# Macaron block (MoE, Mamba, MoE): second MoE phase's row 1 routed inside its row 0, skip term put first, last output row in two halves

## What is computed

```python
x = x + 0.5 * ffn(layernorm(x))
x = x + mamba(layernorm(x))
x = x + 0.5 * ffn(layernorm(x))      # the same weights again

def ffn(x):                          # 16 experts and 2 shared ones, 128 -> 128 -> 128
    scores = sigmoid(x @ router_w.T) # bias, best 2 of 4 groups, best 4 experts in them, weights
    h = einsum('td,edf->etf', x, gate_w)
    u = einsum('td,edf->etf', x, up_w)
    y = einsum('etf,efd->etd', silu(h) * u, down_w)
    return sum_e y[e] * combine[:, e] + shared(x)

def mamba(x):                        # two convolutions with gelu, softplus, 16 states per channel
    h = dA[t] * h + dBu[t]           # scanned along the tokens
    y = sum_n h * C + u * D          # u * D is the skip term
    return concat(y, z) @ W_out
```

## Time and profile before

| | |
|---|---|
| runs | 932.56 us median (931.9 to 933.38) |
| the profiled execution | 931.41 us, its span 929.3 us |
| PE | 887.6 us busy (96%) |
| DVE | 733.9 us busy (79%) |
| POOL | 646.3 us busy (70%) |
| ACT | 576.0 us busy (62%) |
| granted TensorE clock, mean | 0.989 |

### The profile page before, as it was taken

One profiled execution on the slowest core, in us unless ns is written; L12 is line 12 of the kernel. 1 busy time (PEld: TensorE's weight loads), 2 busy tenths in 40 slices (PEclk: granted clock), 3 DMA queues, 4 the chain that ended last, 5 costly groups with the idle time before them and its releaser, 6 DMA issues. The chain is left out here.

```text
span 929.3 us, 12347 instructions
## 1 busy us (share of the span) xinstructions
PE 887.6 (96%) x3655; PEld 632.7 (68%) x3655; DVE 733.9 (79%) x1248; ACT 576.0 (62%) x1022; POOL 646.3 (70%) x471
## 2 busy tenths in 40 slices
PE   8899999999998999999999887789999999999997
PEld 7678778787766665355455433367878878788885
DVE  5969768777975468999999999956877787796664
ACT  6475565565553778888977594136557557555554
POOL 7658666675655456999999887546666667566665
PEclk9999999999999999999999998999999999999999
DMA  7632443333323223334444344243334343334430
GB/s 201 200 123 78 143 121 95 112 118 100 110 84 90 71 81 112 137 118 160 157 154 141 117 136 137 70 141 122 108 111 133 95 134 114 98 102 138 136 112 13
DMA packets 65587, 109.80 MB, mean 118 GB/s; under 512 B 8168, under 2 KB 24688, under 8 KB 65520
## 3 DMA queue, kind: packets, MB, share of 16 engines
q1 hardware_dynamic: 65520, 109.02, 37.5%
HBM read 106.10 MB, written 2.88 MB: 117 GB/s over the span
## 5 line engine op out<-in xcount | busy, mean ns | idle before, releaser
L654 POOL TENSOR_TENSOR act_lo<-act,act_hi 128x512 fp32r<-128x512 f32 x288 | 374.8, 1303 | 237.9 <-ACT act_hi L745 237.4
L738 ACT ACTIVATE bank<-bank 128x512 f32<-128x512 f32 x252 | 146.6, 582 | 234.5 <-PE bank L1035 226.1
L943 DVE TENSOR_TENSOR sg<-bank,c_ring 128x512 f32<-128x512 f32 x252 | 172.6, 685 | 105.0 <-ACT bank L738 103.8
L1031 PE MATMUL bank<-x_parts,w_hi 128*128 128x512 f32 x572 | 235.8, 412 | 9.7 <-DVE act L923 7.1
L923 DVE TENSOR_TENSOR act<-sg,bank 128x512 f32<-128x512 f32 x288 | 197.8, 687 | 48.7 <-PE bank L1035 33.6
L1035 PE MATMUL bank<-x_parts,w_hi 128*128 128x512 f32 x572 | 225.8, 395 | 0.0
L1032 PE MATMUL bank<-x_parts,w_lo 128*128 128x512 f32 x572 | 225.7, 395 | 0.0
L745 ACT ACTIVATE act_hi<-act 128x512 fp32r<-128x512 f32 x288 | 179.4, 624 | 1.2 <-DVE act L923 0.4
L1031 PEld LDWEIGHTS bank<-x_parts,w_hi 128*128 128x128 f32 x572 | 107.8, 188 | 44.7 <-DVE act L923 14.7
L1035 PEld LDWEIGHTS bank<-x_parts,w_hi 128*128 128x128 f32 x572 | 107.7, 188 | 25.4
L1032 PEld LDWEIGHTS bank<-x_parts,w_lo 128*128 128x128 f32 x572 | 108.0, 189 | 24.5 <-issue 2.6
(11 more groups left out here) (182 smaller groups left out, 1049.9 us busy)
## 6 DMA issues: line engine op xcount, KB each, us to landing
c_ring<-c_dram SPq DMA_DIRECT2D x252, 256.0 KB, 3.3
c_ring<-c_dram SPq DMA_DIRECT2D x64, 512.0 KB, 3.7
out<-x_sb SPq DMA_DIRECT2D x8, 256.0 KB, 2.7
x_sb<-in_L_attn_hidden_states SPq DMA_DIRECT2D x3, 512.0 KB, 6.0
stage<-in_L_ffn_gate_w SPq DMA_DIRECT2D x4, 256.0 KB, 4.7
stage<-in_L_ffn_up_w SPq DMA_DIRECT2D x4, 256.0 KB, 4.9
stage<-in_L_ffn_down_w SPq DMA_DIRECT2D x4, 256.0 KB, 5.4
c_dram<-c_rows SPq DMA_DIRECT2D x64, 8.0 KB, 1.9
```

The costliest lines, as they stand in the source:

```text
L654: self.nc.gpsimd.tensor_tensor(m["act_lo"][:, g % LAG], m["act"][:, g % ACTS], m["act_hi"][:, g % LAG].bitcast(FP32), ALU.subtract).then_i ...
L738: nc.scalar.activation(self.s_bank[:, g % 2], self.h_bank[:, g % 2], ACT.Silu).then_inc(self.sg_ready, 1)
L943: nc.vector.tensor_tensor(m["sg"][:, g % 2], silu, weight, ALU.mult).then_inc(self.w_done, 1)
L1031: nc.tensor.matmul(dst, m["w_hi"][:, k, n, :], x_hi, start=True, stop=False)
```

## The change

It does five things. (1) `dve_route(0, 2)` in the Mamba pairs becomes `dve_route(0, 1)`; scores and logits of row 1 leave with it. (2) Row 1 of phase 2 is routed as in phase 1, from block 3 on, with its logits and scores at block 2. (3) The table `SECOND_ROUTE`, now used by both phases, leaves blocks 6, 7 and 10 free and ends at block 16; in phase 2 the statistics of rows 2 and 3 move from block 1 to block 6. (4) The skip term stands before act(1). (5) The last output row is copied, turned, added and stored in two halves.

```diff
                 for g, _ in enumerate(f2.dve_blocks(dve)):
-                    if g == 1:
+                    if g < 2:
                         next(tail)
...
-FRONT_DVE = {41: 1, 43: 1, 45: 1, 54: 2, 55: 2, 56: 2, 57: 2, 58: 2, 59: 1, 60: 1, 61: 1, 62: 1}
+FRONT_DVE = {41: 1, 43: 1, 45: 1, 54: 2, 55: 2, 56: 2, 57: 2, 58: 1, 59: 1, 60: 1, 61: 1, 62: 1}
...
-SECOND_ROUTE = {3 + n: 2 if n < 3 else 1 for n in range(10)}
+SECOND_ROUTE = {3: 2, 4: 1, 5: 1, 8: 1, 9: 1, 11: 1, 12: 1, 13: 1, 14: 1, 15: 1, 16: 2}
...
-    PAIRED = {2: 6, 4: 37, 6: 73}, {2: 1, 4: 37, 6: 73}
+    HALVES = slice(0, SEQ // 2), slice(SEQ // 2, SEQ)
+    PAIRED = {2: 6, 4: 37, 6: 73}, {2: 6, 4: 37, 6: 73}
...
     def rows_before(self, r):
-        if self.p:
-            return r // 2
         return r if r < 2 else 1 + r // 2
...
         if rows is not None:
-            sp.wait_ge(self.x_added, BATCH)
-            sp.dma_start(rows[BATCH - 1], m["x_sb"][:, BATCH - 1]).then_inc(self.stored, 16)
-            sp.wait_ge(self.stored, 16 * BATCH)
+            for n in range(2):
+                tiles = slice(n * TT // 2, (n + 1) * TT // 2)
+                sp.wait_ge(self.x_added, BATCH + n)
+                sp.dma_start(rows[BATCH - 1][:, tiles], m["x_sb"][:, BATCH - 1, tiles]).then_inc(self.stored, 16)
+            sp.wait_ge(self.stored, 16 * (BATCH + 1))
...
-        self.act_scores(ae, 0, 2)
+        self.act_scores(ae, 0, 1)
...
-                if self.p == 0 and g == 2:
+                if g == 2:
                     self.act_scores(ae, 1, 1)
...
     def act_last(self, ae):
-        self.act_read_acc(ae, BATCH - 1)
+        if self.out is None:
+            self.act_read_acc(ae, BATCH - 1)
+            return
+        ae.wait_ge(self.down_done, BLOCKS)
+        ae.wait_ge(self.ot_ready, BATCH - 1)
+        for cols in self.HALVES:
+            self.nc.scalar.activation(self.m["out_t"][:, cols], self.acc[:, cols], ACT.Copy, scale=0.5
+                                      ).then_inc(self.acc_read, 1)
...
-        yield from self.dve_route(dve, 0, 2)
+        yield from self.dve_route(dve, 0, 1)
...
+        for n, cols in enumerate(self.HALVES):
+            x = self.m["x_sb"][:, BATCH - 1].rearrange("p t d -> p (t d)")[:, cols]
+            dve.wait_ge(self.ot_ready, BATCH + n)
+            self.nc.vector.tensor_tensor(x, x, self.last_banks[n][:, 0:SEQ // 2], ALU.add).then_inc(self.x_added, 1)
...
-        routing = self.dve_route(dve, 1, 1) if self.p == 0 else None
+        routing = self.dve_route(dve, 1, 1)
...
-                if self.p == 0 and g == 2:
+                if g == 2:
                     self.pe_logits(pe, 1, 1)
...
     def dve_tail(self, dve):
         self.dve_skip_term(dve, BATCH - 1)
+        yield
         self.dve_add(dve, BATCH - 1)
         yield
```

More of the change, by code:

```diff
@@ L544, in __init__ @@
         self.acc, self.misc = bank[3][:, 0, :], bank[3][:, 1, :]
+        self.last_banks = self.misc, self.h_bank[:, 0, :]
         self.misc_reader = None
@@ L915, in dve_last @@
     def dve_last(self, dve, src):
-        self.dve_add(dve, BATCH - 1, src)
+        if self.out is None:
+            self.dve_add(dve, BATCH - 1, src)
+            return
+        for n, cols in enumerate(self.HALVES):
+            x = self.m["x_sb"][:, BATCH - 1].rearrange("p t d -> p (t d)")[:, cols]
+            dve.wait_ge(self.ot_ready, BATCH + n)
+            self.nc.vector.tensor_tensor(x, x, self.last_banks[n][:, 0:SEQ // 2], ALU.add).then_inc(self.x_added, 1)
     def dve_act(self, dve, g):
@@ L950, in dve_blocks @@
                     self.dve_add(dve, i - 1, self.misc)
+                for _ in range(SECOND_ROUTE.get(g, 0)):
+                    next(routing)
                 if self.p == 0:
-                    for _ in range(SECOND_ROUTE.get(g, 0)):
-                        next(routing)
                     if g in (self.PAIRED[0][2], self.PAIRED[0][4]):
@@ L1016, in pe_down, with pe_transpose_last @@
                          skip_group_check=True).then_inc(self.down_done, 1)
+    def pe_transpose_last(self, pe):
+        nc, m = self.nc, self.m
+        for n, (dst, cols) in enumerate(zip(self.last_banks, self.HALVES)):
+            pe.wait_ge(self.acc_read, BATCH + n)
+            for t in range(TT // 2):
+                last = nc.tensor.transpose(dst[:, t * P:(t + 1) * P], m["out_t"][:, cols][:, t * P:(t + 1) * P], m["ident"][:, :])
+            last.then_inc(self.ot_ready, 1)
     def pe_transpose_out(self, pe, i, dst):
@@ L1074, in pe_front_pieces @@
         yield
-        self.pe_logits(pe, 0, 2)
+        self.pe_logits(pe, 0, 1)
         yield
@@ L1118, in pe_last @@
         self.onto_misc(pe, self.x_added, BATCH)
-        self.pe_transpose_out(pe, BATCH - 1, self.misc)
+        self.pe_transpose_last(pe)
 class Mamba:
```

## The result

The changed kernel takes **926.34 us** (median of four runs, 925.12 to 926.81) where the kernel before took 932.23 beside it: a ratio of 0.9933, 95% interval 0.9916 to 0.9951, so 6.2 us less (4.6 to 7.8); the two medians are 5.9 apart. Its profiled execution took 925.93 us with a span of 924.1, against 931.41 and 929.3. 923.5 was forecast: the sign and the range held, the size was 2.8 us too large.

The account below looks back on a forecast made before the run. PE bounds 616 to 918 us, DVE the last Mamba pairs. Terms -2.8 - 2.55 - 2.33 - 1.8 + 0.8 - 0.4 = -9.1 from the profiled 931.41 give 922.3; plus 1.15 to the median, 923.5, range 921 to 927.

Parts of the forecast that it names:

- Phase 1: Row 0 of phase 1: PE's six stalls waiting for DVE's acts shrink, gaining 2.8 us, from 1.8 to 3.4.
- if it meets nothing in its new place: Phase 1, row 0: piece 5, moved behind act(8), runs undelayed there, so act(9) starts at 40.1.
- Mamba pairs: Last Mamba pairs: routing one row instead of two shortens DVE's work, 2.3 us plus 0.25 for logits, 2.55 in all.
- rival 3: Mamba pairs: saved time isn't passed on because POOL or PE at lower clock sets the pace; loses 2, 925.5; chance 0.08.
- The idle 2.33: Between Mamba and phase 2: the skip term ahead of act(1) removes PE's idle time, gaining 2.33 us.
- Its clock: Projection behind the idle time: PE's granted clock no longer falls, gaining 1.8 us, or 0 if it falls all the same.
- rival 1: Projection between Mamba and phase 2: PE's clock stays down; gain 7.3, time 925.3; chance 0.18.
- Phase 2: Row 0 of phase 2: row 1's logits and route pieces give back 0.8 us, with 0.5 of stall, from 0 to 2.5.
- rival 2: Route pieces meet POOL in phase 2's blocks 3 to 6, also phase 1; waits cost 2.5 to 3, 926.0; chance 0.12.
- The end: Last output row in halves: stages overlap and the last store comes earlier, gaining 0.4 us, from 0 to 0.7.
- Weights of row 1: Phase 1: turned at block 16 instead of 12, their loads stay hidden by 1 us, cost 0.
- Rival 4: Slower: POOL waits at nearly all 13 groups in both phases, 9 us of PE stall each; 936 at worst; chance 0.04.

Follow-up runs that it names:

- experiment 9: Changed kernel with DVE's second low part of the weights three blocks later in phase 1's row 0, behind block 11: 926.5 us, 0.9926.
- experiment 6: Changed kernel with row 1's logits and scores at Mamba pairs 57 and 58 and phase 2's route begun from block 0: 925.9 us, 0.9921.
- experiment 1: Kernel before with only the new SECOND_ROUTE table in phase 1: 931.02 us, 0.9979.
- experiment 2: Kernel before with only the last Mamba row's skip term put ahead of act(1): 930.28 us, 0.9965.
- experiment 8: Changed kernel with GpSimd's low part of the activations cut to 8 columns in phase 2's row 0, so not computing all: 924.75 us, 0.991.
- experiment 3: Kernel before with only the last output row copied, turned, added and stored in two halves: 932.85 us, 0.9992.
- experiment 4: Changed kernel without the move of row 1's route, both rows routed in the Mamba pairs: 925.92 us, 0.9925.
- changed, again: Changed kernel run once more with no edit: 927.22 us, 0.9935 of the kernel before.
- experiment 7: The kernel of experiment 6 run once more on another occasion: 924.99 us, 0.9921.
- both (10): Changed kernel with the edits of experiment 6 and experiment 9 together: 927.38 us, 0.9929.
- experiment 11: Changed kernel with an added zero-weight matmul between the two state additions of Mamba pairs 44 to 55: 929.44 us, 0.9961.
- lighter (12): Kernel of experiment 6 with a 128-column zero-sum matmul between the two state additions of pairs 44 to 61: 927.64 us, 0.9935.

## Why the prediction was right, and where it was not

The sign and the range held. The steps:

- **Phase 1, 2.8 forecast: 2.0 to 2.2 measured** (act(17) and act(120), twice), inside 1.8 to 3.4. Of five stalls 0.3 us is left in sum; the sixth kept 2.05 of the 1.2 to 2.3 left to it. u(11)'s first matmul came 1.77 us earlier, below the 2.1 to 3.2 that I gave it: "if it meets nothing in its new place" did not hold, the pieces met GpSimd at 31 and at 38 us. Moving DVE's low part (experiment 9) does not mend the stall; a phase 1 without these waits was not run.
- **Mamba pairs, 2.55 forecast: 2.7 to 3.1.** Changed kernel -0.40 to -3.09 from scan 53 to 63, its second execution -0.12 to -3.25, experiment 6 -0.07 to -2.89. All of it was passed on, so rival 3 falls. The last scan came 3.1 us earlier and not 5.3, by the 1.8 at pair 53 and the 0.6 that phase 1 was short.
- **The idle 2.33: 2.56**, the stall with its restart (experiments 1 and 2).
- **Its clock, 1.8: this step failed.** "What stood before the fall here was idle time that goes" made one execution's clock a property of the program. Two kernels with the same 2.33 us of idle time had clock 1.00 behind it. Of three executions with the old order one has this low stretch. By adding 1.15 us to come from that execution to the median I carried a gain over to the other executions, and of the two more of them that are profiled neither had the loss. The profiled execution of the changed kernel had in turn 1.8 us more at scan 53 than that of the kernel before. Without this step the forecast would have been 925.3, rival 1's time, though for another reason than its own: the clock did not stay down.
- **Phase 2, 0.8 back: 2.3.** The place was right (u(6) after act(4), 0.36 us to spare, and it came 0.83 late), the size was not. This is rival 2, whose waits I priced at 2.5 to 3 in sum: three instructions lost 1.14, 0.99 and 0.4 us (L818, L846, L844). Experiment 8 takes 1.7 of the 2.3 away by cutting GpSimd's half of the meeting down. By my own numbers two full meetings of 1.03 past the 0.36 us to spare make 1.7, what experiment 8 took away; I had them in the rival and not in the term.
- **The end, 0.4: 0.6.** Experiment 3, by its rows; its runs (0 to 1.6 us) could not tell it from 0.
- **Weights of row 1: hidden**, as forecast by 1 us; experiment 9 shows the wait when they are 1.7 us later.

Rival 4's 936 does not follow from its own 18 us of stall, which on top of 923.5 make 941; neither came near.

The range held for its width: it was made to reach rivals 1 to 3, and the time came out 0.3 us from rival 2's 926.0, with its waits in phase 2 alone and without the gain in the projection's clock.

With the measured terms the sum is -2.1 - 2.7 - 2.6 + 2.3 - 0.6 = -5.7 us, inside the measured 4.6 to 7.8. The single edits sum to the same: 2.0 (table) + 3.3 (skip term) + 0.7 (halves) = 6.0, and the route move adds -2.7 + 2.3, nothing that can be told. Open is a drift of 0.3 to 0.5 us between act(26) and act(143) in the changed kernel and experiments 3 and 4, with no wait to its name.

## What to carry to other kernels

Moving work of the engine that sets the pace to a later stretch pays only if it keeps no other engine waiting there: here 2.7 us were taken out of one stretch and 2.3 put into the next, and the three small edits (table, skip term, halves) brought the whole gain. Before a low clock is counted as the price of a stall, find it in a second execution of the same program. Small VectorE instructions with two SBUF inputs should be priced with GpSimd's schedule beside them, and placed where no act stands close behind.

## What the runs showed of the hardware

**The low clock moves.** The stretches, in steps of 2 us, with a granted clock of at most 0.8 in each profiled execution (us from the start; the last 5 us are left out):

```
before            550-554, 572-578, 584-588, 612-616
changed           548-556, 570-574, 582-586
changed, again    294-298, 550-554, 584-588
table             44-48, 296-300, 552-560, 572-576, 582-594
skip term first   296-300, 552-560, 572-576, 584-588
halves            298-302, 536-540, 558-560, 574-578, 588-596
no route move     44-48, 296-300, 552-560, 572-576, 582-594
early route       294-298, 550-554
early, again      294-298, 550-554
small low         42-46, 534-538, 554-558, 572-576, 584-588
low part later    294-298, 550-554, 584-588
both (10)         294-298, 550-558, 572-576, 586-588
more work (11)    42-46, 296-298
lighter (12)      294-298, 570-574, 584-592
```

The stretch between 294 and 302 us costs 1.3 to 1.6 us wherever it appears (act(120) to act(126) in the table of offsets), and one at 42 to 48 us about 1.5. The one around pair 53 moves the scan by 1.7 to 2.0 us against the kernel before where it lasts beyond 554 us ("small low" with its 4 us too), and by 0.1 to 0.5 where it ends at 554 (scans 51 to 53 of "again" and "early"), as it does in the kernel before. The stretch at 42 to 48 us stands in four of eleven executions with row 1's pieces in new places and in none of the three with the old ones. In all four it comes right behind the one long stall (some 2.05 us), which the other five with the same table have too; whether the table brings it is open, and if it does, the table is worth less than 2.1. The busy time by stretch at that pair, in experiment 2, which is the kernel before up to there, and in the kernel before:

```profile
552.00:554.00 2.00, 1.98 (x3) 0.84 (x4) 2.00 (x1) 2.00 (x5) 1.20 (x2) 0.67 0.17 70
554.00:556.00 2.00, 1.37 (x3) 0.18 (x2) 1.91 (x3) 2.00 (x5) 1.86 (x2) 0.50 0.64 225
556.00:558.00 2.00, 2.00 (x7) 1.73 (x8) 1.84 (x2) 2.00 (x4) 2.00 (x2) 0.50 0.00 0
```

```profile
550.00:552.00 2.00, 1.74 (x3) 0.89 (x4) 2.00 (x2) 2.00 (x4) 1.23 (x2) 0.72 0.14 55
552.00:554.00 2.00, 1.49 (x2) 0.00 (x0) 1.91 (x3) 2.00 (x5) 1.86 (x2) 0.50 0.78 250
554.00:556.00 2.00, 1.97 (x9) 1.40 (x10) 2.00 (x2) 2.00 (x4) 2.00 (x2) 0.93 0.01 4
```

From 544 to 592 us PE is busy 76 to 81% of the time in the changed kernel (the rows of experiment 11), with gaps of about a microsecond. What sets where the clock falls within that is open: experiment 11 shows only that it stayed up there with more work of PE, in one profiled execution; the mean clock of its six executions is 0.995 to 0.999, that of the changed kernel's nine 0.988 to 0.996. The Trainium skill (TensorE: Matmul & The Clock Gate, "HAM oscillation — how this bites in real kernels") has idle gaps as what lowers the clock. Idle time of 2.33 us, from 609.8 us on in the kernel before and some 3 us later in experiments 1 and 3, stood ahead of a low stretch in the first and not in the other two, so in this trace the gap alone does not decide it.

**Single executions of one program differ by up to 3.9 us** (experiment 7: six of 924.49 to 928.43), as much as two or three such stretches cost. That is as much as the largest edit of this change is worth.
